# Post-norm sequence block on one core: the two batches' router searches put out of step

## The reference, cut to what matters

```python
# first layer
a = tanh(x @ WA.T); b = x @ WB.T                    # N = 16
g = sigmoid(x @ Wg.T + bg); dx = x @ WD.T + bD
h[t] = a[t] * h[t-1] + b[t]                         # scan over the sequence
x = layernorm(x + (h @ WC.T) * g + dx * (1 - g))
# second layer
weights = x @ router_w + router_b
topv, topi = top_k(weights, S // 8)                 # 512 of 4096
sel_idx = sort(topi[:, :511])
x_sel, w_sel, pos = x[sel_idx], weights[sel_idx], position_ids[sel_idx]
m_sel = attention_mask[:, 0][sel_idx, sel_idx]      # rows, then columns
hn = rmsnorm(x_sel, ln1)
q, k = rope(heads(hn @ wq), pos), rope(heads(hn @ wk), pos)   # 16 heads of 16
o = softmax(q k^T / 4 + m_sel) v @ wo
x1 = x_sel + o
x2 = x1 + gelu(rmsnorm(x1, ln2) @ w1) @ w2          # F = 1024
out = zeros.at[sel_idx].set(x2 * w_sel) + x * (1 - sel_mask)
return layernorm(x + out)
```

## Time and profile before

| | before |
|---|---|
| median of the runs, us | 534.05 (533.18 to 535.07) |
| the profiled execution's own time, us | 536.87 |
| its span, us | 535.0 |
| TensorE busy | 449.4 us, 84% |
| VectorE busy | 391.9 us, 73% |
| ScalarE busy | 291.8 us, 55% |
| POOL busy | 173.5 us, 32% |
| mean granted TensorE clock | 0.926 |

### The profile page before, as it was taken

The page is one execution under the profiler, slowest core; times in us unless marked ns, Lnnn a source line. Parts: engine busy times, 40 slices in busy tenths (PEclk is TensorE's granted clock), DMA queues, the critical chain, the costliest instruction groups (busy, mean ns, idle before and its releaser), DMA issues.

```text
span 535.0 us, 10439 instructions
## 1 busy us (share of the span) xinstructions
PE 449.4 (84%) x3410; PEld 334.2 (62%) x3410; DVE 391.9 (73%) x1216; ACT 291.8 (55%) x615; POOL 173.5 (32%) x210
## 2 busy tenths in 40 slices
PE   3699999898999342798879999998998999997970
PEld 2477888786887232666657666674785666663560
DVE  2687898798898688848379999938459999937050
ACT  2244646444655260016879999915678999932200
POOL 9146667676767620470241000001000000002232
PEclk9999999998999855579998999998999999997995
DMA  8613342342231210186620000000000000000100
GB/s 257 191 41 80 104 133 80 116 121 79 80 118 41 78 40 1 42 261 250 235 80 2 4 0 1 1 2 0 1 1 0 4 1 0 2 3 10 31 29 11
DMA packets 29846, 33.85 MB, mean 63 GB/s; under 512 B 6340, under 2 KB 25448, under 8 KB 29800
## 3 DMA queue, kind: packets, MB, share of 16 engines
q1 hardware_dynamic: 23024, 24.78, 14.4%
q0 software_dynamic: 3520, 8.40, 5.1%
q10 hardware_dynamic: 3256, 0.10, 0.4%
HBM read 19.63 MB, written 13.63 MB: 62 GB/s over the span
## 4 chain that ended last, share of the span: by engine, by line
PE 39%; DVE 13%; issue 12%; POOL 9%; ACT 5%; DMA 1%; POOLq 1%; DVEq 0%; ACTq 0%
PE ps L896 9%; PE ps L912 6%; PE ps L966 6%; PE ps L883 5%; PE ps L973 4%; POOL arena L489 3%; PE ps L833 3%; PE ps L852 2%; POOL r L498 2%; POOL h_parts L548 1%; PE ps L837 1%; PE ps L859 1%; POOL rq L503 1%; DVE arena L1380 1%; ACT arena L1174 1%
## 5 line engine op out<-in xcount | busy, mean ns | idle before, releaser
L1174 ACT ACTIVATE arena<-arena,nmax 128x511 f32<-128x511 f32 x128 | 92.0, 720 | 7.7 <-DVE nmax L1587 6.8
L1587 DVE CUSTOM_DVE_ANT_0 arena<-ps,nmask 128x511 f32<-128x511 f32 x128 | 84.7, 683 | 0.5 <-DVE nmask L1535 0.2
L896 PE MATMUL ps<-ident,arena 128*128 128x128 f32 x512 | 79.8, 279 | 3.7 <-DVE big L394 1.3
L896 PEld LDWEIGHTS ps<-ident,arena 128*128 128x128 f32 x512 | 60.5, 142 | 24.6 <-ACT arena L1174 15.0
L621 POOL COPY arena<-v_sb 128x256 f32<-128x256 f32 (+1 forms) x8 | 3.2, 399 | 152.2 <-PE ps L912 152.1
L680 PE MATMUL ps<-wgd_hi,x_hi 128*128 128x512 f32 x128 | 51.9, 405 | 0.0
L394 DVE COPY big<-ps 128x512 f32<-128x512 f32 x64 | 44.0, 688 | 9.8 <-PE ps L896 9.3
L883 PE MATMUL ps<-arena 96*128 (+1 forms) x128 | 49.1, 389 | 2.1 <-DVE nmask L1535 1.1
L681 PE MATMUL ps<-wgd_lo,x_hi 128*128 128x512 f32 x128 | 50.6, 395 | 0.0
L682 PE MATMUL ps<-wgd_hi,x_lo 128*128 128x512 f32 x128 | 50.6, 395 | 0.0
L489 POOL TENSOR_TENSOR arena<-arena 128x512 f32<-128x512 f32 x32 | 41.4, 1295 | 12.4 <-DVE arena L1280 10.8
(11 more groups left out here) (233 smaller groups left out, 978.4 us busy)
## 6 DMA issues: line engine op xcount, KB each, us to landing
arena<-in_L_attn_x SPq DMA_DIRECT2D x16, 512.0 KB, 4.6
out<-ob_sb SPq DMA_DIRECT2D x16, 512.0 KB, 3.2
w_sb<-in_L_ffn_w SPq DMA_DIRECT2D x2, 1024.0 KB, 10.5
mt_scratch<-nmask SPq DMA_DIRECT2D x8, 256.0 KB, 2.7
mt_scratch<-big SPq DMA_DIRECT2D x8, 256.0 KB, 3.1
big<-in_L_attn_Wg SPq DMA_DIRECT2D x1, 256.0 KB, 4.2
big<-in_L_attn_WD SPq DMA_DIRECT2D x1, 256.0 KB, 4.9
wqk<-in_L_ffn_wq SPq DMA_DIRECT2D x1, 256.0 KB, 7.8
```

The costliest lines, as they stand in the source:

```text
L896: mm = pe.transpose(ps[:, 2 + u % 2, k * P:(k + 1) * P], pr[u % 4][:, k * P:(k + 1) * P], ident[:, :])
L1174: act.activation(pr[u % 4][:, 0:K - 1], sm[u % 4][:, 0:K - 1], ACT.Exp, bias=nmax[:, c, h:h + 1], scale=-1.0, accum_out=rsum[:, c, h:h + 1 ...
L1587: dve.tensor_tensor_reduce(sm[u % 4][:, 0:K - 1], ps[:, S_BANKS[u % AHEAD], 0:K - 1], nmask[b][:, c, 0:K - 1], 1.0, 3.4e38, ALU.add, ALU.m ...
```

## The change

- *First stage.* Batch 0's search begins in batch 1's part of it. In groups 10 to 16 VectorE makes one `narrow` and one `compare` of batch 0 between the products of the second half and the first half's statistics (two rounds in the last), and TensorE one `count` after a group's second transposes. The router's row is read from SBUF (`rw_row`) and no longer from PSUM, mean and variance lie in SBUF (`mean_var`), so PSUM bank 1 is free for the counts.
- *After the first stage:* last narrowing, mark, slots and one-hots of batch 0, and only then batch 1's logits and first comparison. Batch 1's eight rounds, its slots and one-hots stand among batch 0's normalisation, rope and parts on VectorE and among its projections, mask turns and splits on TensorE. There is one buffer of high one-hots for both batches.
- *Batch 1's projections* move from before the first attention to between the attentions, with its mask rows' turns and its first normalisation. Its gathers of x and mask rows are issued by POOL after the first turn of the first attention.
- v is copied by ScalarE (`copy_v`), not VectorE. Mask rows of batch 0 are turned block by block; the DRAM scratch is stored in the same order. Banks, buffers and semaphores follow these moves (`hnT2` is the turned second norm in `onT`'s memory).

```diff
@@ -53,7 +53,8 @@
 M_STORES = MS // P
 AHEAD = 4
 S_BANKS = (0, 1, 6, 7)
-M_BANKS = (4, 6, 5, 7)
+M_BANKS = (2, 3)
+SPLIT_BANK = (4, 0)
...
+        mean_var = [sb(f"mean_var{j}", [P, T, 2]) for j in range(2)]
...
+        hnT2 = onT[:, 0:KD, :]
...
+        m_rows = [m[:, 0:C * MS].rearrange("p (c s) -> p c s", c=C) for m in (big, qk_all)]
+        m_k = [arena2[:, 2048:4096].rearrange("p (c k) -> p c k", c=C), qk[0]]
...
+                if G >= NG + 2:
+                    count(0, G - NG - 2)
...
+            count(0, 6)
+            count(0, 7)
+            flag_sums(0)
+            pick_rows(0)
+            count(1, 0)
+            pick_rest(0)
+            count(1, 1)
+            count(1, 2)
+            for c in range(2):
+                turn_first_hn(0, c)
+            for c in range(C):
+                project(0, range(c, c + 1))
+                if c < C - 1:
+                    count(1, 3 + c)
+                if c + 2 < C:
+                    turn_first_hn(0, c + 2)
+            turn_mask_block(0, 0)
+            count(1, 6)
+            turn_mask_block(0, 1)
+            count(1, 7)
+            turn_mask_block(0, 2)
+            flag_sums(1)
+            turn_split(0, 0)
+            turn_mask_block(0, 3)
+            pick_rows(1)
+            turn_split(0, 1)
             pick_rest(1)
-            for c in range(1, C):
-                if c + 1 < C:
-                    turn_first_hn(0, c + 1)
-                project(0, range(c, c + 1))
-            turn_mask_rows(0)
+            turn_split(0, 2)
+            turn_split(0, 3)
+            for c in range(C):
+                turn_mask_columns(0, c)
+            attention(0)
+            pe.wait_ge(onT_ready, TURNS)
+            for c in range(C):
+                project_out(0, c, range(TURNS - 1, TURNS))
+            for c in range(C):
+                turn_mask_block(1, c)
             for c in range(2):
                 turn_first_hn(1, c)
-            for c in range(2):
+            for c in range(C):
+                if c == C - 1:
+                    turn_hn(0)
                 project(1, range(c, c + 1))
-                turn_first_hn(1, 2 + c)
-            turn_mask_rows(1)
-            pe.wait_ge(mT_ready[1], MS // P)
+                if c + 2 < C:
+                    turn_first_hn(1, c + 2)
+            hidden(0)
             for c in range(C):
-                turn_split(0, c)
-                if c < 2:
-                    project(1, range(2 + c, 3 + c))
-            turn_mask_columns()
-            for b in range(B):
-                attention(b)
-                pe.wait_ge(onT_ready, (b + 1) * TURNS)
-                for c in range(C):
-                    project_out(b, c, range(TURNS - 1, TURNS))
-                if b == 0:
-                    turn_second_mask_columns()
-                    pe.wait_ge(nm_ready[1], 2)
-                turn_hn(b)
-                pe.wait_ge(nm_ready[1], C)
-                hidden(b)
-                for c in range(C):
-                    if b < B - 1 and c == C - 1:
-                        turn_split(b + 1, c)
-                    second_product(b, c)
-                    if b < B - 1 and c < C - 1:
-                        turn_split(b + 1, c)
+                if c == C - 1:
+                    turn_split(1, c)
+                second_product(0, c)
+                if c < C - 1:
+                    turn_split(1, c)
+                turn_mask_columns(1, c)
+            attention(1)
+            pe.wait_ge(onT_ready, B * TURNS)
+            for c in range(C):
+                project_out(1, c, range(TURNS - 1, TURNS))
+            turn_hn(1)
+            hidden(1)
+            for c in range(C):
+                second_product(1, c)
...
+            def copy_v(b, c):
+                act.wait_ge(v_done[b], c + 1)
+                act.copy(v_sb[b][:, c, :], ps[:, 6 + c % 2, 0:D]).then_inc(v_ready[b], 1)
...
+            copy_mask_block(0, 0)
+            copy_mask_block(0, 1)
+            more_parts(0, 0)
+            copy_mask_block(0, 2)
+            copy_turned(0, 0)
+            copy_mask_block(0, 3)
+            for c in range(1, C):
+                more_parts(0, c)
+                copy_turned(0, c)
             sines(1)
...
+                    pool.wait_ge(rows_ready[1], 3)
+                    gather_x(1)
+                    pool.wait_ge(e_parts, 2 * C)
+                    gather_mask_rows(1)
+                kept(b)
...
-                    step.done(dve.tensor_tensor_reduce(junk[:, t, :], s_sb[j][:, t, :], ps[:, 1, 0:D], 1.0, 0.0,
+                    step.done(dve.tensor_tensor_reduce(junk[:, t, :], s_sb[j][:, t, :], rw_row[:, :], 1.0, 0.0,
...
-                mv = ps[:, 1, AGGR + 2 * T * j:AGGR + 2 * T * (j + 1)].rearrange("p (t m) -> p t m", t=T)
+                mv = mean_var[j]
...
                     products(G - 1, 1)
+                    if G >= NG + 2:
+                        if G > NG + 2:
+                            narrow(0, G - NG - 3)
+                        compare(0, G - NG - 2)
                     half_statistics(G - 1, 0)
+                    if G == NGB:
+                        narrow(0, 6)
+                        compare(0, 7)
...
-            logits(1)
-            for r in range(ROUNDS):
-                for b in range(B):
-                    if r:
-                        narrow(b, r - 1)
-                    compare(b, r)
-            for b in range(B):
-                narrow(b, ROUNDS - 1)
-            for b in range(B):
-                mark(b)
-            slots(0)
-            one_hots(0)
-            slots(1)
-            rows(0)
-            one_hots(1)
-            factors(0)
...
+            narrow(0, 7)
+            mark(0)
+            slots(0)
+            one_hots(0)
+            logits(1)
+            compare(1, 0)
+            rows(0)
+            narrow(1, 0)
+            compare(1, 1)
+            factors(0)
             angles(0)
-            for c in range(2):
+            narrow(1, 1)
+            compare(1, 2)
+            for c in range(C):
                 first_normalised(0, c)
+            narrow(1, 2)
+            compare(1, 3)
+            cosines(0)
+            rope(0, 0)
+            narrow(1, 3)
+            compare(1, 4)
+            rope(0, 1)
+            narrow(1, 4)
+            compare(1, 5)
+            parts(0, 0)
+            narrow(1, 5)
+            compare(1, 6)
+            rope(0, 2)
+            narrow(1, 6)
+            compare(1, 7)
+            rope(0, 3)
+            narrow(1, 7)
+            mark(1)
+            slots(1)
+            parts(0, 1)
+            one_hots(1)
+            copy_turned(0, 0)
+            parts(0, 2)
             rows(1)
+            copy_turned(0, 1)
+            parts(0, 3)
+            factors(1)
+            angles(1)
+            copy_turned(0, 2)
+            copy_turned(0, 3)
+            copy_mask()
+            attention(0)
+            for c in range(C):
+                first_normalised(1, c)
+            residual(0)
+            mean_square(0, 3, 4)
+            cosines(1)
+            rope(1, 0)
+            rope(1, 1)
+            normalised(0)
+            parts(1, 0)
+            rope(1, 2)
+            parts(1, 1)
+            rope(1, 3)
+            copy_turned(1, 0)
             for c in range(2, C):
-                first_normalised(0, c)
-            factors(1)
-            cosines(0)
-            for c in range(C):
-                value(0, c)
-                rope(0, c)
-                if c == 0:
-                    angles(1)
-                if c == 1:
-                    parts(0, 0)
-                if c == 2:
-                    for n in range(C):
-                        first_normalised(1, n)
-            parts(0, 1)
-            for c in range(2):
-                value(1, c)
-            for c in range(C):
-                copy_turned(0, c)
-                if c < 2:
-                    parts(0, 2 + c)
-                    value(1, 2 + c)
-            copy_mask()
-            for b in range(B):
-                attention(b)
-                residual(b)
-                mean_square(b, 3, 4)
-                normalised(b)
-                if b < B - 1:
-                    cosines(b + 1)
-                    for c in range(C):
-                        rope(b + 1, c)
-                    split(b + 1)
-                    add_second(b, range(C))
+                parts(1, c)
+                copy_turned(1, c - 1)
+            copy_turned(1, C - 1)
+            add_second(0, range(C))
+            attention(1)
+            residual(1)
+            mean_square(1, 3, 4)
+            normalised(1)
```

350 lines of the change are left out of this document (170 added, 180 removed).

## The result

The changed kernel takes 542.98 us (median of four runs, 542.01 to 543.68), beside 534.43 us for the kernel before on the same chip (the three runs on record with the prediction, 534.05, and a fourth): ratio 1.0162, 95% interval 1.0134 to 1.0189. That is +8.6 us where +3.5 was forecast. The direction and the range held; the size of the change was more than twice the forecast.

The account below looks back on a forecast made before the run. Bounds: POOL and VectorE taking turns in the first stage, VectorE's chain in the router's search, TensorE between the attentions. 17 - 21.7 - 5.6 + 13.8 = +3.5 on the median: 537.5 us, range 524 to 546.

Parts of the forecast that it names:

- the clash: First stage: VectorE operations with two SBUF inputs wait for POOL's SBUF operations, each meeting costing up to a whole POOL operation.
- First stage, groups without a round: Nine first-stage groups without a search step: dots held by POOL cost 0.65 us each, 5.9 us of the stage's +17.
- First stage, groups with a round: Groups 10 to 15: a 1.14 us search round plus 0.65 for held dots, six times, 10.8 us of the stage's +17.
- To the row numbers: From the last statistics to batch 0's row numbers: 10.2 us needed instead of 31.9, so -21.7 us.
- To the first scores: From batch 0's row numbers to the first scores: 54.3 us for 59.9, so -5.6 us (-15 to +4).
- the clock step: Before the first scores: TensorE's clock low again for some 8 us, worth 3 us.
- Rival B: Before the first scores: TensorE stays at 1.2 GHz through the mixed phase, +4 instead of -5.6, total 547.2 us; chance 0.15.
- Between the attentions: Between the attentions: batch 1's mask rows, turns of hn and four projections moved in, +13.8 us (+12 to +16.8).
- The sum on the median: Whole kernel: +3.5 us, summed against the profiled execution (536.87), put on the runs' median (534.05), gives 537.5 us.
- Rival A: VectorE is not held by POOL: first stage costs 5.0, clock recovers at once, total 522.5 us; chance 0.18.
- its partial form: Partial clash in the first stage: dots held, rounds in idle time, +9 there, total 529.5 us; chance 0.13.
- C: A buffer or store holds the gathers or second search; about 8 of 21.7 us come back, 545.5 us; chance 0.04.

Follow-up runs that it names:

- before_dots_sbuf: The kernel before with one edit, the dots read the router's row from SBUF: 555.50 us, 1.018 of the kernel before.
- after_again: The changed kernel, unchanged, run again on a chip where the kernel before takes 543.55 us: 548.83 us, ratio 1.010.
- dots_psum: The changed kernel with dots reading the router's row from PSUM (all groups but the last) and TensorE's count at a group's end: 540.58 us, 0.990 of the kernel before.
- best_moved_end: The changed kernel with dots from PSUM, search rounds behind the group's last statistics and TensorE's count behind the gate products: 527.95 us, 0.986 of the kernel before.
- picks_later: The changed kernel with batch 1's one-hots and picks behind batch 0's parts on VectorE and splits on TensorE: 551.05 us, 1.014 of the kernel before.
- warm_fill: The changed kernel with 124 extra matmuls where TensorE waits for VectorE before the first scores: 552.29 us, 1.011 of the kernel before.
- before_again: The kernel before, unchanged, profiled on a chip where it takes longer: 544.98 us, beside 543.55 us for the kernel before there.

## Why the prediction was right or wrong

*What bounds the kernel, and the clash.* Right. Dots read from SBUF wait for POOL (1.51 for 0.41), and before_dots_sbuf shows it alone. By the Trainium skill's rule on the shared ports ("SBUF — State Buffer", "SBUF: two separate sides") the later of two such instructions waits for the whole of the other. The trace agrees with it for POOL's 512-wide operations; beside POOL's power operations, which read SBUF too, a comparison with two SBUF inputs took its free 0.41 us, and there the measurement decides.

*First stage, groups without a round.* There are ten of them, not nine (the stage has 16 groups, the sum has 15), and they lost 6.8 us, where nine at 0.65 made 5.9. The price was right, about 0.6 in most of them; the working was not: I let both dots go before L489, and in fact the second is the one that waits and POOL is not delayed. One group, 51.38 to 62.60, also ran at a clock of 0.93 and took 11.2 us (10.1 in after_again).

*First stage, groups with a round.* The step that failed is "1.14 + 0.65 = 1.8, six times": 10.8 us. The six groups lost 13.7, 2.3 a group. Their lengths, from one of POOL's L507 (its place in each kernel) to the next:

| group | before | dots_psum | after |
|---|---|---|---|
| 10 | 10.93 | 13.05 | 13.07 |
| 11 | 9.45 | 11.59 | 12.97 |
| 12 | 9.43 | 11.35 | 11.37 |
| 13 | 9.56 | 11.30 | 11.32 |
| 14 | 9.24 | 10.73 | 10.75 |
| 15 | 9.28 | 11.76 | 12.16 |
| sum | 57.9 | 69.8 | 71.6 |

With the dots free (dots_psum) the rounds alone cost 11.9 us, 2.0 a group where the sum has 1.14; the dots add 1.9 where the sum has 3.9. So it is the round that was mis-sized. I had named the held round as the upper bound and priced the likeliest case without it, though the row on L1312 spoke for it as much as for the dots: the comparison took 970 ns on average where 407 is free. And I counted six rounds where the stage holds eight comparisons and seven narrowings: the first comparison falls in group 9, and the last group has two of each. In the profiled execution group 11 is 1.4 us longer than in dots_psum at a clock of 0.93 for 1.00; in after_again it is group 12. Of this step's lower bound, 5.0 for a round that nothing holds, best_moved_end comes close: 190.8 - 185.5 = 5.3 us for all the rounds, once most of them stand where POOL runs its power operations.

*To the row numbers.* -21.7 for -21.7, and the gathers did not wait.

*To the first scores.* -2.8 for -5.6. VectorE's work was right within 1 us (45.4 for 44.4), the clock step wasn't: I had 8 us at half clock, and it was low (0.67 to 0.82) again from 240 on, where TensorE has counts, mask turns, picks and splits, in part with waits between them. The second split of batch 0 takes 3.63 us (1.95 for such a row between the attentions), and the second pick stands in front of the next one:

```profile
256.41 3.63 PE L859 MATMUL ps<-ident_b,arena 128*96 128x128 bf16 x32
259.83 3.54 PE L766 MATMUL ps<-hn,onT 128*128 128x52 bf16 x32
```

Rival B did not come true as it stands: clock 0.5 did not last past half of the stretch (its mean is 0.76), and the stretch is not 4 us longer but 2.8 shorter. But part of what it names is there. Order (picks_later) and fillers (warm_fill) did not win the missing 2.8 us back, so how much of them is the clock's stays open.

*Between the attentions.* +12.0 for +13.8: the mask rows' turns with their copies (354.22 to 359.02, 4.8 for 4.5) and the four projections (about 2.6 each) came as counted. The turns of hn were sized too high (about 1.1 us ahead of the projections, and not 2.0), and those of the second norm, which took 2.03 us in rows 9, take 1.19 now.

*The sum on the median.* I put a sum made on one execution on the median of others. The profiled execution of before was 2.4 us above its median, with 80.1 us in the first attention at a clock of 0.98 (79.1 at 1.00 in before_again) and 44.5 between the attentions (43.7). These 2 us made the old kernel look slower than it mostly is. Of the miss of 5.1 us, 3.5 are the first stage's, 2.8 the stretch before the first scores, 1.8 this; 1.8 between the attentions and 1.2 in the attentions and the tail went the other way.

*Rival A* fell with the held dots of the trace (1.51 us), and its partial form with the 11.9 us of the rounds, which were not in idle time. *C* fell too: the row numbers came 10.2 us after the last statistics.

## What to carry to other kernels

Before an operation is moved next to another engine's, look in the trace for one small instruction that stands beside both: if its duration depends on the neighbour, price everything of its kind as held, the moved work included. When a piece of a chain is moved on one engine, move what waits for it on the others too: where TensorE's count stood moved the end of the stage by 19 us (209.7 and 190.8) with the same round on VectorE. And overlap is measured against the overlap that was already there: two searches taking turns cost 8.0 us for seven rounds, the first stage as changed 10.9, and only the last version less, 5.3.

## What was not expected of the hardware

The instructions that POOL holds are not only those with two tensors in SBUF: L1379, one 128x32 bf16 tensor and a number per partition, took 1.15 us beside L499 and 0.23 free. POOL's power operations held nothing here: the comparison of 480 columns ran in 0.41 us wholly beside one (161.98 and 161.42 in best_moved_end).

The same kernel before has two lengths on different chips, 534 to 535 and 544 to 546 us, and the long one (before_again) has idle times of VectorE and ScalarE (15.7 and 10.8 us) while gathers run that the short one has not at that length. In the change that stretch is as short there as on the first chip, and the first attention is 5.7 us longer instead. That fits its being 1.6% slower on one chip and 1.0% on the other; what delays the engines stays open.
